# A state-space layer and a mixture of experts on one core: the product of time step and x moved behind the norm's sums, the next expert's rows transposed between an expert's two layers, the one-hot work cut into eighths, and the last normalization shared out anew

## The reference, cut to what matters

```python
# state-space layer: 512 inner channels, 16 states
dA = exp(soft_clamp(dt[..., None] * A))
dB = dt[..., None] * Bp[:, :, None, :]
def step(h, inp):
    h = h * dA_t + dB_t * x_t[:, :, None]          # dB_t * x_t = (dt * x) * B
    nrm = sqrt(sum(h * h, axis=(1, 2)))
    fac = minimum(20.0 / (nrm + 1e-08), 1.0)
    h = where(t % 10 == 0, h * fac, h)             # every tenth step
    y = einsum('bdn,bn->bd', h, C_t) + D_param * x_t
x = layernorm(x + x + scale * (y * silu(gate)) @ W_out.T)
# mixture of experts: each token to its two best experts
expert_in = zeros(E, C, D).at[e_flat, p_flat].add(contrib)
h = relu(einsum('ecd,edh->ech', expert_in, w1) + b1)
expert_out = einsum('ech,eho->eco', h, w2) + b2
y = sum(tok * gate, axis=1)
x = layernorm(x + y)
```

## Time and profile before

| | us |
|---|---|
| median of three runs | 2886.46 |
| the profiled execution | 2887.04 |
| its span on the core | 2885.2 |
| busy DVE / PE / ACT / POOL | 2434.5 / 2642.1 / 2274.4 / 2155.9 |
| state-space phase, about | 0 to 2392 |
| choice of experts and one-hot work | 2392 to 2455 |
| experts | 2455 to 2829 |
| last scatter, last norm and output | 2829 to 2885 |

### The profile page before, as it was taken

One profiled execution on the slowest core, in us unless ns is written; L12 is line 12 of the kernel. 1 busy time (PEld: TensorE's weight loads), 2 busy tenths in 40 slices (PEclk: granted clock), 3 DMA queues, 4 the chain that ended last, 5 costly groups with the idle time before them and its releaser, 6 DMA issues. The chain is left out here.

```text
span 2885.2 us, 51759 instructions
## 1 busy us (share of the span) xinstructions
PE 2642.1 (92%) x16812; PEld 2403.8 (83%) x16812; DVE 2434.5 (84%) x3452; ACT 2274.4 (79%) x5161; POOL 2155.9 (75%) x2239
## 2 busy tenths in 40 slices
PE   5899999999999999999999999999999884899992
PEld 4899999999999999999999999999999874576761
DVE  1999999999999999999999999999999986112113
ACT  6999999999999999999999999999999922111113
POOL 1788888888888888888888888888888862423315
PEclk8999999999999999999999999999999986999996
DMA  1222222222222222222232222222222212323216
GB/s 59 67 75 79 78 71 79 78 69 82 71 80 77 75 76 78 73 80 70 77 81 72 79 77 75 77 78 73 80 70 79 72 51 85 81 59 99 60 43 244
DMA packets 153973, 225.73 MB, mean 78 GB/s; under 512 B 46056, under 2 KB 92776, under 8 KB 152552
## 3 DMA queue, kind: packets, MB, share of 16 engines
q1 hardware_dynamic: 131208, 188.98, 22.3%
q0 software_dynamic: 9216, 12.59, 2.5%
q10 hardware_dynamic: 13280, 20.86, 2.1%
HBM read 189.26 MB, written 33.05 MB: 77 GB/s over the span
## 5 line engine op out<-in xcount | busy, mean ns | idle before, releaser
L642 POOL TENSOR_TENSOR H<-H,CB 128x640 f32<-128x640 f32 x832 | 1236.1, 1499 | 224.0 <-DVE H L479 223.9
L479 DVE TENSOR_TENSOR_SCAN H<-DA,PM 128x704 f32<-128x704 f32 x832 | 1317.1, 1604 | 1.3 <-ACT DA L276 1.3
L394 ACT ACTIVATE DA<-DT,SM 128x160 f32<-128x160 f32 x3328 | 1115.9, 424 | 1.5 <-POOL DT L610 0.3
L664 PE MATMUL YB<-H,ID 128*128 128x160 f32 x6656 | 1050.5, 310 | 0.2 <-POOL H L642 0.2
L664 PEld LDWEIGHTS YB<-H,ID 128*128 128x128 f32 x6656 | 989.0, 192 | 16.4 <-issue 11.2
L454 DVE TENSOR_TENSOR PM<-PM,BB 128x640 f32<-128x640 f32 x832 | 678.7, 816 | 5.8 <-DMA BB<-Bd 0.7
L276 ACT ACTIVATE DA<-DA 128x2560 f32<-128x2560 f32 x208 | 485.4, 2334 | 1.7
L1121 POOL DMA_INDIRECT YA<-YS,IG x48 | 75.2, 1566 | 239.9 <-ACT YS L944 228.4
L621 POOL TENSOR_TENSOR FC<-SN,HALF 128x4 f32<-128x4 f32 x206 | 212.4, 1031 | 31.2 <-DVE SN L485 23.2
L765 PE MATMUL PZ<-WO,Z 128*80 128x256 f32 x832 | 188.5, 380 | 0.1
L1177 PE MATMUL PE<-XTE,W 128*128 128x384 f32 x512 | 169.1, 492 | 10.1 <-issue 9.2
(11 more groups left out here) (164 smaller groups left out, 3993.7 us busy)
## 6 DMA issues: line engine op xcount, KB each, us to landing
BB<-Bd SPq DMA_DIRECT2D x208, 320.0 KB, 3.4
CB<-Cd SPq DMA_DIRECT2D x208, 320.0 KB, 3.3
W<-in_w ACTq DMA_DIRECT2D x16, 1024.0 KB
XT<-in_xT SPq DMA_DIRECT2D x52, 160.0 KB, 2.2
XR<-in_xp SPq DMA_DIRECT2D x416, 20.0 KB
X2d<-VV SPq DMA_DIRECT2D x416, 20.0 KB
YA<-VV SPq DMA_DIRECT2D x416, 20.0 KB
HI<-YA SPq DMA_DIRECT2D x6, 1024.0 KB, 9.9
```

The lines of the kernel that those rows point to most:

```text
L394: eng.activation(DA[:, c0:c0 + 2, :, a, m, 1:11].rearrange("p c b t -> p b c t"), DT[:, j % 2, a].rearrange("p b (c t) -> p b c t", c=2), ...
L479: eng.tensor_tensor_scan(H[:, q % 3, u], a0, DBX(u), 0.0, ALU.mult, ALU.add).then_inc(s_scan, 1)
L642: eng.tensor_tensor(h, h, cb, ALU.mult).then_inc(s_hc, 1)
L664: mm = eng.matmul(yv, ID[:], hv[:, :, :, n, 0:10], start=False, stop=n == 15)
```

## The change

Four edits. (1) `dt_x(2i+1)` moves from slot 4 to slot 2 of its block, and `dt_x(2i+2)`, which was at slot 0 of the next block, to slot 6; both now stand behind `norm_sum` and ahead of a `scan`. (2) The one-hot work goes in 8 parts of 8 columns. (3) The transposes of expert e+1 stand on PE between the layers of expert e, with `XTE` in two buffers, their copies on DVE behind the evacuations of layer 1; layer 1 waits for two of three copies and for the third only at its second piece. (4) The 8 rows of the last norm go 6 to ACT, 1 to POOL, 1 to DVE (4, 2 and 2 for the last sequence).

```diff
-                    if live and s == 0:
-                        dt_x(2 * i)
-                    if live and s == 4:
-                        dt_x(2 * i + 1)
...
                     if u == 2 and 1 <= q <= NQ - 2:
                         norm_sum(q - 1)
+
+                    if s == 2 and live:
+                        dt_x(2 * i + 1)
+                    if s == 6 and ok(i + 1):
+                        dt_x(2 * i + 2)
                     if live:
                         scan(q, u)
...
-        XT = sb("XTE", [128, 2, 768])
+        XT = sb("XTE", [128, 2, 2, 768])
...
-        LO = sb("LO", [128, 2, 2, 16, 128])
+        LO = sb("LO", [128, 2, 2, 8, 128])
...
+        def shares(b):
+            return (6, 7) if b < B - 1 else (4, 6)
...
-            for c in range(4):
-                j = slice(16 * c, 16 * c + 16)
+            for c in range(8):
+                j = slice(8 * c, 8 * c + 8)
...
+            def turn(e):
+
+                if e >= E:
+                    return
+                if e >= 2:
+                    eng.wait_ge(s_h, 16 * (e - 1))
+                for c in range(3):
+                    eng.wait_ge(s_xt, 3 * e + c + 1)
+                    eng.tensor_copy(XT[:, e % 2, :, 256 * c:256 * c + 256],
+                                    bank(turned(e, c))[:].rearrange("p (a n) -> p a n", a=2)).then_inc(s_xtc, 1)
...
+            def normed(b):
+
+                eng.wait_ge(s_nm, b + 1)
+                for j in range(shares(b)[1], 8):
+                    eng.tensor_scalar(rows(b)[:, j], rows(b)[:, j], SD[:, b, j:j + 1], NM[:, b, j:j + 1],
+                                      ALU.mult, ALU.add).then_inc(s_x3v, 1)
...
+                if b > 0:
+                    normed(b - 1)
+            normed(B - 1)
...
+            turn(0)
+            for e in range(E):
                 eng.wait_ge(s_wl[e % 2], 32 * (e // 2 + 1))
-                eng.wait_ge(s_xtc, 3 * (e + 1))
+                eng.wait_ge(s_xtc, 3 * e + 2)
                 for m in range(8):
                     for h in range(2):
-                        n = k + 3 + 2 * m + h
+                        n = hidden(e, m, h)
+                        if (m, h) == (0, 1):
+                            eng.wait_ge(s_xtc, 3 * e + 3)
...
+                turn(e + 1)
                 eng.wait_ge(s_hr, 8 * (e + 1))
                 eng.wait_ge(s_hv, 8 * (e + 1))
```

More of the change, by code:

```diff
@@ L900, in sync_program @@
                 o = out[L * b:L * b + L, :].rearrange("(p j) n -> p j n", p=128)
-                for j0, j1, done, n in ((0, 5, s_x3a, 5), (5, 8, s_x3p, 3)):
-                    eng.wait_ge(done, n * (b + 1))
-                    eng.dma_start(o[:, j0:j1], rows(b)[:, j0:j1]).then_inc(s_out, 16)
+                ja, jp = shares(b)
+                eng.wait_ge(s_x3a, 6 * b + ja)
+                eng.dma_start(o[:, 0:ja], rows(b)[:, 0:ja]).then_inc(s_out, 16)
+                eng.wait_ge(s_x3p, b + jp - ja)
+                eng.wait_ge(s_x3v, b + 8 - jp)
+                eng.dma_start(o[:, ja:8], rows(b)[:, ja:8]).then_inc(s_out, 16)
             eng.wait_ge(s_out, 32 * B)
@@ L926, in scalar_program @@
             eng.wait_ge(s_rt, RT_G)
-            for c in range(4):
+            for c in range(8):
                 eng.wait_ge(s_eq[0], c + 1)
-                for j in range(16 * c, 16 * c + 16):
+                for j in range(8 * c, 8 * c + 8):
                     eng.activation(HI[:, 0, j, 0:48], HI[:, 0, j, 48:96], ACT.Copy,
@@ L949, in scalar_program @@
                 x = rows(b)
-                for j in range(5):
+                for j in range(shares(b)[0]):
                     eng.activation(x[:, j], x[:, j], ACT.Identity, bias=NM[:, b, j:j + 1],
@@ L1135, in gpsimd_program @@
                 eng.wait_ge(s_nm, b + 1)
-                for j in range(5, 8):
+                for j in range(*shares(b)):
                     eng.tensor_scalar(x[:, j], x[:, j], SD[:, b, j:j + 1], NM[:, b, j:j + 1],
@@ L1151, in tensor_program, with turn @@
                     eng.wait_ge(s_gate[n], c + 1)
-                    for j in range(16):
-                        t = eng.matmul(GP, LO[:, c % 2, n, j], HI[:, n, 16 * c + j], start=(c, n, j) == (0, 1, 0),
-                                       stop=(c, n, j) == (3, 0, 15))
+                    for j in range(8):
+                        t = eng.matmul(GP, LO[:, c % 2, n, j], HI[:, n, 8 * c + j], start=(c, n, j) == (0, 1, 0),
+                                       stop=(c, n, j) == (7, 0, 7))
                     t.then_inc(s_gi, 1)
             eng.wait_ge(s_rt, RT_IX)
-            for e in range(E):
-                k = 22 * e
+            def turn(e):
+                if e >= E:
+                    return
                 for c in range(3):
-                    if k + c >= 8:
-                        done, n = evacuated(k + c - 8)
-                        eng.wait_ge(done, n)
+                    n = turned(e, c)
+                    if n >= 8:
+                        eng.wait_ge(*evacuated(n - 8))
                     eng.wait_ge(s_xe[e % 2][c], 32 * (e // 2 + 1))
```

62 lines of the change are left out of this document (34 added, 28 removed).

## The result

The changed kernel takes 2821.09 us (median of four runs, 2820.67 to 2821.85) where the kernel before takes 2886.42 (four runs, 2884.79 to 2888.19): a ratio of 0.9774, 95% interval 0.9757 to 0.9791. The profiled execution took 2820.67 us with a span of 2818.9.

What follows compares the result with a forecast made beforehand. DVE bounds the state-space phase, PE with two holes per expert the expert phase, POOL's queue the last norm. 31.2 + 1.9 + 0.8 + 14.6 + 5.5 = 54.0 us off 2887.04 gives 2833.0, as median 2832; range 2822 to 2851.

Steps and rivals of the forecast that it cites:

- I take 0.60: 52 x 0.60 = 31.2 us: State-space phase: moving the two products shortens each of 52 blocks by 0.60 us, between DVE's 0.66 and ACT's 0.55.
- its 0.66: State-space block, DVE: the two products cost 0.96 us in their new places instead of 1.62, saving 0.66.
- ACT's side: State-space block: ACT waits for DVE at slot 12's square (0.17) and the gate's tanh (0.38), so can give about 0.55 us.
- The wait in slot 6: State-space block: the moved product waits 0.16 us for POOL's state product to end, so costs 0.56 us instead of 0.40.
- 7 x (1.32 + 0.76) = 14.6 us: Expert phase: both PE holes, 1.32 us before layer 1 and 0.76 before layer 2, go at seven borders.
- The one-hot work (1.8 against 1.9): Choice of experts: halved parts shorten DVE's lead before PE's one-hot matmuls, saving 1.9 us; bounds 0 and 2.2.
- the first hole (1.0 against 0.8): First expert: layer 1 no longer waits 0.88 us for the third copy, saving 0.8 us.
- The last norm gave 4.9 against 5.5: End of kernel: POOL, with one row instead of three, keeps pace with DVE, saving 5.5 us; bounds 2 and 7.
- the output's queue: Last norm: DMAs keep the end from coming before 2878 or so, 7 us sooner; output waits in the queues at times.
- ACT did not hold the block: Rival, state-space block: ACT bounds it, only 0.29 us a block is saved, 15.1 instead of 31.2, 2849 us; chance 0.16.
- POOL's power never went first: Rival, slots 2 and 6: the product waits 1.03 us for POOL's power; 2936 us, slot 6 alone 2883; chance 0.03 each.
- The last norm did not turn: Rival, last norm: DVE's new row waits for POOL's power each time, 9.8 us later, total 2842 us; chance 0.12.

## Why the prediction was wrong

The direction, the four places and what each edit does were right; the sum was 11 to 12 us short, and 8.3 of them lie in one term.

*"I take 0.60: 52 x 0.60 = 31.2 us"* is the step that failed. DVE's side gave more than its 0.66 and ACT's side did not hold at 0.55.

- ACT. I added up two waits from one page of the timeline and called that what ACT could give. Five extra instructions put 0.85 us a block on ACT of the kernel before and nothing changed; three in the changed kernel showed 0.25 to 0.28 us left beside the 0.77 to 0.79 already used. So ACT had 1.0 to 1.1. Three of the missing pieces can be seen: at the head of the block 0.10 us idle and 0.09 of overlap ahead of L296; PE's answer to ACT there (L305), waited for 1.15 us before and 1.05 after; and about 0.1 ahead of the tanh at 1039. The list of waits shows none of them as something ACT could give. Why PE's answer came sooner, perhaps because XN is undisturbed, was not tested, and up to 0.1 us was not located.
- The wait in slot 6. I charged 0.16 us from the product's start to POOL's recorded end. The same rows of before held the answer: at slot 4 the product ended 0.35 us behind POOL's end, though alone it takes 0.49. A start up to 0.14 us ahead of POOL's end therefore costs nothing, and 0.15 ahead waits 0.01. I had written down the 0.35 and did not use it.

With both terms right the sum would have been 52 x 0.80 = 41.6; 39.5 came, since the mean block gave 0.77 and not 0.80.

*"7 x (1.32 + 0.76) = 14.6 us"* was mis-sized: a border gave 2.54. The holes' idle time was read right; the 0.24 us behind each was not counted, though the prediction took such an overlap into account for DVE and ACT. 7 x 0.46 = 3.2 us. The rest of that stretch's 19.2, 1.3 us, is the first layer 1 (21.56 against 22.90). The prediction had no term for it; by the table above it came, in the main, with the earlier rise of the clock.

The one-hot work (1.8 against 1.9) and the first hole (1.0 against 0.8) came as worked out. The last norm gave 4.9 against 5.5: DVE's row cost 0.30 us from start to start instead of 0.27, and the output's queue, named as the other limit, held the end.

The rivals. ACT did not hold the block. POOL's power never went first: of the 92 products from 200 to 2200 us none took more than 0.53 us, and where the two met the power grew from 1.03 to 1.25 us. The last norm did not turn; DVE reached its row at the head of POOL's small operations, and POOL's first one took 0.27 instead of 0.20. The range was cut too short at its low end by the same limit of ACT: with 0.80 a block in place of 0.66 it would have gone down to 2820 and held the result.

## What to carry to other kernels

An engine that is "100% busy" can be waiting inside its instructions. Compare the durations of one instruction form on one shape: where the least is 0.48 us and the most 1.14, look for another engine's operation that ends where the long ones do, and move the instruction to a place where that engine is about to wait for you, or give it an input from PSUM.

Do not take an engine's listed waits for all it can give. Gaps of 0.1 us and lost overlaps are in no list and here made up a good part of it; a dummy instruction in each iteration measures the slack directly. And a hole costs what it shows plus the overlap lost behind it.

## What the runs showed of the hardware that was not expected

- A DVE product with both inputs in SBUF that was held up by POOL ended 0.35 to 0.36 us after the recorded end of POOL's operation in three places, begun 0.20, 0.76 and 0.93 us before that end; alone it takes 0.49. A start 0.15 us ahead of POOL's end cost nothing that can be read (0.50 and 0.51 us).
- When DVE's product and POOL's next operation stood ready together, DVE's went first each time, also between two operations of POOL that follow each other without a gap: in slot 4 of the kernel before, where POOL's pair took 3.18 us instead of 2.91, and at 2261, where POOL's power took 1.28 instead of 1.03. At slot 0 of the kernel before XN is recorded as begun 0.08 us before DVE's product, and still took 1.28 instead of 0.86 while the product took 0.49.
- PE's work behind an idle time is longer by 0.19 us (transposes, 1.50 against 1.31) and 0.24 us (layers), at a granted clock of 1.00 on both sides of the hole.
- After an idle stretch the moment at which the clock rises from 1.2 to 2.4 GHz (granted 0.50 to 1.00) differs by more than a microsecond between executions, with the same code too: it rose 3 to 7 us after the start of the one-hot matmuls, which took 30.5 to 32.1 us in the runs. The rows below are the first expert's first layer: the first of the kernel before (layer begun at 2467.73, still at 0.50 four microseconds later), the second of the changed one (begun at 2425.50, at 0.93 in the stretch from 1.5 us on). Up to the choice of experts too, profiles of kernels with the same code there lie 2.8 us apart (2356.1 and 2358.9). Single profiles of this kernel are not comparable to better than some 3 us.

```profile
2470.20:2471.70 1.50, 1.50 (x4) 0.68 (x3) 0.00 (x0) 0.58 (x1) 1.20 (x2) 0.50 0.34 112
```
```profile
2427.00:2428.50 1.50, 1.50 (x5) 0.77 (x4) 0.00 (x0) 0.58 (x1) 1.20 (x2) 0.93 0.28 87
```
